# A chain of 1/sqrt moved from GpSimd to VectorE, with GpSimd's row scatters issued in one run

## Chip, cores and metric

One core of a Trainium2 chip. The metric is the device time of one execution in microseconds; the number shown for a kernel is the median of its runs.

## What is computed

The input x is 8 sequences of 512 tokens of 256 values. All of the work starts from xn, the layer norm of x (no gain or bias).

- Recurrence branch: q = xn Wq, v = xn Wv; a state per channel, state[t] = lam * state[t-1] + v[t] with lam = sigmoid(beta) per head; y = q * state; **layer norm of y over its 256 channels, (y - mean) / sqrt(var + 1e-5)**, then gain ln_g and bias ln_b; times silu(xn Wg); times Wo. Its result is s.
- Expert branch: a router picks 2 of 8 experts for each of the 4096 tokens, with softmax weights; each expert is silu(a) * b of a 256 to 1024 projection, then 512 to 256. The sum and a bias go through silu. Its result is g.
- Output: x + s * g.

The change is about the 1/sqrt of the norm in bold.

## The kernel before

One program drives five engines by hand: each engine has its own list of instructions (a queue in program order) and waits on semaphores of the others. Products are split in f16 high and low parts, three matmuls each (L944). A chunk is one sequence: 4 tiles of 128 tokens; CH = 8 chunks. The work has three stages.

**First**, x is loaded and normed in eight groups (the inverse roots of these norms come from GpSimd's `rstd`, L367 to L374, and stay there in both kernels), the router chooses experts, and VectorE works out for each token and each of its two experts a row of a buffer in memory, `slots_dram`. GpSimd then writes the normed rows there: 64 indirect DMAs of 128 rows (`scatter`, L398 to L406; the DMA is L403). The second half of them waits for `routed` to reach 2.

**The early recurrence** runs chunks 0 to 5 (EARLY = 6). Each engine has a function `recur(c)`, chunks 0 and 1 written out and 2 to 5 in a loop:

- VectorE (L791): the scan over 512 steps from PSUM (L798, two instructions), y = q * state (L806), the product with the gate of the chunk before and its low part (`times_gate`, L841 and L844, two instructions each), the statistics of y (`bn_stats` L818, `bn_aggr` L825, which raises `y_var`), in chunk 1 the list of expert blocks (`list_blocks`, L769 to L785), and the low parts of four pieces of expert weights (L832).
- ScalarE (L578): gain and bias of the chunk before (L548), high part of its product (L557), silu of the gate (L586), four weight pieces (L561), then, once `y_rstd` is there, the norm of y from PSUM into z (L597, four instructions), which raises `z_ready`, and the copy of the finished s (L566).
- TensorE: the projections, the transposes of y (L1045) and of z (L1012), the output projection of the chunk before.
- SyncE loads the weight pieces, fills the padding of `slots_dram`, and then waits for `pads_filled` and for all 64 scatters before the first slot load (L309).
- GpSimd works off its scatters and stops for each chunk's root. This order is written out by hand:

```
done = SCATTERS_FIRST
scatter(0, done)
for c in range(EARLY):
    if c >= 1:
        pool.wait_ge(z_ready, c)
    rstd(0, y_var, c + 1, y_rstd)
    end = min(done + SCATTERS_EACH, N_SCATTERS)
    scatter(done, end)
    done = end
```

SCATTERS_FIRST is 14 and SCATTERS_EACH is 11. `rstd` is four small operations on 128x4 elements (L370 to L373; L372 is the power -0.5) and writes the scale and the offset that L597 reads.

**The expert blocks**: 39 blocks of 256 rows, each loaded from `slots_dram` by SyncE, transposed and split (L608 on ScalarE, L854 on VectorE), put through its expert by TensorE, and scattered by GpSimd into `y_dram` (L449). Block 0 needs all 24 weight pieces (L832) and its own L854. VectorE also waits for all 64 row scatters ahead of its first L854.

**The tail** runs chunks 6 and 7 of the recurrence, now without weight pieces, while SyncE loads the experts' results in eight loads of 1 MB (L333). Sums of the two results per token: GpSimd for chunks 1 to 4 (`sum_y`, L477), VectorE for 0, 5, 6 and 7 (L900). ScalarE takes silu (L576), VectorE the product with s (`finish`, L907 and L912), and x is added by GpSimd for chunks 0 to 5 (`add_x`, L473), by VectorE for 6 and 7 (L919). SyncE stores each chunk. On GpSimd the order in the tail is: root of chunk 6, the four sums, root of chunk 7, the six adds. On VectorE: recur(6), L900 and L907 of chunk 0, recur(7), L907 of 1 to 3, L900 of 5 and 6, `times_gate`, the rest.

Lines of the kernel that the change and the prediction touch: L369 to L373, L403, L409 to L417, L477, L480 to L485, L473 on GpSimd; L798, L806, L818, L825, L832, L841, L844, L900, L907 on VectorE; L597 on ScalarE.

Of the kernel before, what the change touches and what calls it, by code (L numbers as in the profile page):

```python
# [33 lines left out]
P = 128  # L34
# [4 lines left out]
TPC = S // P  # L39
CH = B  # L40
# [28 lines left out]
N_SCATTERS = TOPK * NT  # L69
SCATTERS_FIRST = 14  # L70
SCATTERS_EACH = 11

# [9 lines left out]
def build(nc, x, wq, wv, wg, wo, beta, ln_g, ln_b, router, w_exp, bias, out):  # L82
    ctx = ExitStack()
    with ctx:
        def sb(name, shape, dt=F32):
            return ctx.enter_context(nc.sbuf_tensor(name, shape, dt))

        def sem(name):
            return ctx.enter_context(nc.semaphore(name))
# [108 lines left out]
        cols = sb("cols", [P, 4, KD])  # L198
        neg_half = sb("neg_half", [P, TPC])
        spare = sb("spare", [P, 7])  # L200
        bn = [sb(f"bn{i}", [P, TPC, 6]) for i in range(AHEAD)]
# [19 lines left out]
        def slots_ps_of(b, i):  # L221
# [30 lines left out]
            sem, ("sil_ready", "g_ready", "g_hi_ready", "g_split"))  # L252
        meta_ready = sem("meta_ready")
        y_scattered = [sem(f"y_scattered{i}") for i in range(2)]
# [89 lines left out]
        def _(pool):  # L344
# [63 lines left out]

            done = SCATTERS_FIRST  # L409
            scatter(0, done)  # L410
            for c in range(EARLY):
                if c >= 1:
                    pool.wait_ge(z_ready, c)
                rstd(0, y_var, c + 1, y_rstd)
                end = min(done + SCATTERS_EACH, N_SCATTERS)
                scatter(done, end)
                done = end  # L417

# [56 lines left out]
            def sum_y(c):  # L475
                pool.wait_ge(y_loaded[c], 16)
                pool.tensor_tensor(res[c], y_in[c][:, :, 0, :], y_in[c][:, :, 1, :], ALU.add)\  # L477
                    .then_inc(pool_sum, 1)

            for c in range(EARLY, CH):  # L480
                pool.wait_ge(z_ready, c)
                rstd(0, y_var, c + 1, y_rstd)
                if c == EARLY:
                    for early in SUMS_POOL:
                        sum_y(early)  # L485
            for c in range(X_POOL):
# [159 lines left out]
        def _(dve):  # L646
# [142 lines left out]
            dve.wait_ge(lam_ready, 1)  # L789

            def recur(c, convert=True, buffers=early_buffers):  # L791
                states, _, _, _ = buffers
# [31 lines left out]
                for j in range(TPC):  # L824
                    last = dve.bn_aggr(mv[0][:, j, :], bn[0][:, j, :])  # L825
                last.then_inc(y_var, 1)
                if isinstance(c, int) and c == 1:
                    list_blocks()
# [339 lines left out]
```

## Time and profile before

| | |
|---|---|
| median of 3 runs | 570.37 us (569.82 to 572.63) |
| span of the profiled execution | 547.8 us |
| the profiled execution's own time | not given with the profile; the runs are 22.0 to 24.8 us above the span |
| busy share of the span | TensorE 85%, VectorE 60%, GpSimd 50%, ScalarE 41% |
| mean granted TensorE clock | 0.945 |
| row scatters (L403) | 64, 74.0 us busy |
| chain that ended last, by engine | issue 32%, GpSimd 23%, TensorE 17%, DMA 16%, VectorE 7% |

The span is from the first to the last instruction. Busy counts the time in which an engine executes an instruction; waits on semaphores, register work and the issue of DMAs do not count. A length of an instruction in the timeline holds the time that it waits for a port. An engine's idle time before an instruction is put down to what ended it ("[6.53 <-POOL stat L373]"). "issue" is time in which the engine waited for nothing that the profile shows.

### The profile page before, as it was taken

To read this page: it belongs to the slowest core of one execution; us is meant where nothing else is said; L and a number is where in the kernel's file an instruction comes from. 1 tells how busy PE (TensorE), PEld (TensorE's weight loads), DVE (VectorE), ACT (ScalarE), POOL (GpSimd) and SP (SyncE) were. 2 spreads that over 40 slices of the span, in tenths; PEclk is the share of its full clock that TensorE was granted. 3 is DMA by queue.
4 is the path that set the end of the run, shared out by engine and by line. 5 is a ranking of instruction groups with operands and counts; after the bars stand their busy time and mean duration, and the time that the engine had idled before them with its cause. 6 is when DMAs were issued, how large, how long until landed. Compare 5 with 4: busy or idle time off the path is not lost.

```text
span 547.8 us, 13251 instructions
## 1 busy us (share of the span) xinstructions
PE 466.4 (85%) x3896; PEld 377.0 (69%) x3897; DVE 326.6 (60%) x583; ACT 224.5 (41%) x354; POOL 273.9 (50%) x547
## 2 busy tenths in 40 slices
PE   1866668679689899999999999999999999999521
PEld 1753345344468788888888888888888888866321
DVE  4998896578635444554544545545445455448976
ACT  4963337455753333333332433423324333316450
POOL 4617887878722434344343443443444434445784
PEclk9999797799889999999999999999999999999756
DMA  8803659565440324312122121121221211019644
GB/s 261 276 4 108 221 175 313 218 228 176 150 143 20 106 83 153 96 45 68 52 73 58 58 66 58 56 68 48 76 58 56 74 57 39 20 44 370 242 153 153
DMA packets 42051, 64.69 MB, mean 118 GB/s; under 512 B 5037, under 2 KB 30768, under 8 KB 42032
## 3 DMA queue, kind: packets, MB, share of 16 engines
q1 hardware_dynamic: 33408, 46.34, 26.9%
q0 software_dynamic: 6816, 16.92, 8.7%
q10 hardware_dynamic: 1808, 1.19, 0.7%
q8 instruction: 9, 0.15, 0.1%
q14 instruction: 10, 0.08, 0.0%
HBM read 40.93 MB, written 25.33 MB: 121 GB/s over the span
## 4 chain that ended last, share of the span: by engine, by line
issue 32%; POOL 23%; PE 17%; DMA 16%; DVE 7%; POOLq 2%; ACT 2%; DVEq 0%; SPq 0%; ACTq 0%
DMA y_dram<-rows_raw 13%; POOL slots_dram L403 9%; PE bankC L944 5%; PE bankB L944 5%; PE bankA L944 4%; POOL stat L372 2%; POOL y_dram L449 2%; DMA w_raw<-x_in 2%; DVE w_raw L841 1%; POOL rows_raw L436 1%; POOL rows_raw L440 1%; POOL spare L432 1%; PE bankD L1012 1%; POOL rows_raw L428 1%; POOL spare L447 1%
## 5 line engine op out<-in xcount | busy, mean ns | idle before, releaser
L944 PE MATMUL bankA<-rows_raw,w_raw 128*128 128x256 f16 x936 | 110.2, 275 | 2.0 <-DVE rows_raw L854 2.0
L944 PE MATMUL bankC<-w_raw,rows_raw 128*128 x936 | 109.2, 273 | 0.4 <-DVE rows_raw L862 0.3
L944 PE MATMUL bankB<-rows_raw,w_raw 128*128 128x256 f16 x936 | 108.6, 273 | 0.0
L944 PEld LDWEIGHTS bankA<-rows_raw,w_raw 128*128 x936 | 92.0, 99 | 14.1 <-issue 2.7
L944 PEld LDWEIGHTS bankC<-w_raw,rows_raw 128*128 128x128 f16 x936 | 90.0, 98 | 14.3 <-issue 2.6
L944 PEld LDWEIGHTS bankB<-rows_raw,w_raw 128*128 x936 | 91.5, 98 | 10.3
L449 POOL DMA_INDIRECT y_dram<-rows_raw x78 | 79.2, 1015 | 32.8 <-issue 32.8
L403 POOL DMA_INDIRECT slots_dram<-rows_raw,pos_i x64 | 74.0, 1156 | 30.9 <-issue 20.1
L862 DVE TENSOR_TENSOR rows_raw<-rows_raw 128x512 f16<-128x512 f32 x78 | 54.0, 693 | 55.7 <-ACT rows_raw L622 55.7
L859 DVE SCALAR_TENSOR_TENSOR rows_raw<-rows_raw,bankA 128x512 f32<-128x512 f32 x39 | 26.8, 687 | 92.9 <-ACT rows_raw L617 92.9
L617 ACT ACTIVATE rows_raw<-bankA 128x512 f32<-128x512 f32 x39 | 23.3, 597 | 128.5 <-PE bankA L944 128.5
L622 ACT ACTIVATE rows_raw<-rows_raw 128x512 f16<-128x512 f32 x78 | 49.1, 630 | 60.2 <-DVE rows_raw L859 60.2
L447 POOL TENSOR_TENSOR spare<-spare 128x1 f32<-128x1 f32 x39 | 7.5, 192 | 100.1 <-DVE rows_raw L872 100.1
L428 POOL TENSOR_TENSOR rows_raw<-rows_raw,blk_e 128x2 f32<-128x2 f32 x39 | 7.2, 186 | 62.1 <-DMA y_dram<-rows_raw 62.1
L872 DVE SCALAR_TENSOR_TENSOR rows_raw<-bankC,rows_raw 128x256 f32<-128x256 f32 x78 | 34.2, 479 | 4.9 <-PE bankC L944 3.8
L1012 PE MATMUL bankD<-ident,work 128*128 128x128 f32 x64 | 13.5, 381 | 27.2 <-ACT work L597 27.2
L859 DVE SCALAR_TENSOR_TENSOR rows_raw<-rows_raw,bankB 128x512 f32<-128x512 f32 x39 | 26.8, 687 | 16.0 <-ACT rows_raw L617 16.0
L617 ACT ACTIVATE rows_raw<-bankB 128x512 f32<-128x512 f32 x39 | 23.3, 597 | 24.0 <-PE bankB L944 24.0
L597 ACT ACTIVATE work<-bankD,stat 128x256 f32<-128x256 f32 x32 | 15.4, 563 | 41.2 <-POOL stat L373 41.2
L1012 PEld LDWEIGHTS bankD<-ident,work 128*128 128x128 f32 x64 | 10.9, 197 | 30.3 <-ACT work L597 29.9
L832 DVE SCALAR_TENSOR_TENSOR w_raw<-work,w_raw 128x1024 f32 (+1 forms) x24 | 27.6, 1212 | 0.0
L854 DVE TENSOR_TENSOR rows_raw<-bankD,rows_raw 128x512 f16<-128x512 f32 x38 | 26.0, 683 | 0.2 <-ACT rows_raw L608 0.2
(151 smaller groups left out, 670.4 us busy)
## 6 DMA issues: line engine op xcount, KB each, us to landing
work<-w_exp_in SPq DMA_DIRECT2D x24, 512.0 KB, 5.2
rows_raw<-slots_dram SPq DMA_DIRECT2D x39, 260.0 KB
w_raw<-y_dram SPq DMA_DIRECT2D x8, 1024.0 KB, 14.1
w_raw<-x_in SPq DMA_DIRECT2D x9, 512.0 KB, 4.2
out<-w_raw SPq DMA_DIRECT2D x8, 512.0 KB, 2.9
work<-x_in SPq DMA_DIRECT2D x7, 512.0 KB, 4.6
slots_dram<-fill SPq DMA_DIRECT2D x9, 260.0 KB, 4.9
y_dram<-rows_raw POOLq DMA_INDIRECT x78, 2.4
```

The costliest lines, as they stand in the source:

```text
L403: pool.indirect_dma_start(out=slots_dram, out_offset=bass.IndirectOffsetOnAxis(slot, 0), in_=row, in_offset=None, bounds_check=SLOTS - 1, ...
L449: pool.indirect_dma_start(out=y_dram, out_offset=bass.IndirectOffsetOnAxis(dest[i][:, s:s + 1], 0), in_=ys[i][:, s, :], in_offset=None, bo ...
L597: last = act.activation(z[:, j, :], bankD[:, j // 2, j % 2 * D:j % 2 * D + D], ACT.Identity, bias=stat[0][:, 2, j:j + 1], scale=stat[0][:, ...
L617: act.activation(sil[j], AB[j][:, :, 0:BLOCK], ACT.Silu, scale=1.0 / WSCALE).then_inc(sil_ready, 1)
L622: act.activation(g_hi[i][:, 2 * j:2 * j + 2, :], g32[j], ACT.Copy)\
L832: dve.scalar_tensor_tensor(w_lo[:, piece], wst[:, i % STAGES, :], WSCALE, w_hi[:, piece], ALU.mult, ALU.subtract).then_inc(w_lo_ready, 1)
L854: dve.tensor_tensor(xT[i][:, KD:2 * KD, :], slots_ps_of(b, i), xT[i][:, 0:KD, :], ALU.subtract).then_inc(slot_lo_ready, 1)
L859: dve.scalar_tensor_tensor(g32[j], sil[j], 1.0 / WSCALE, AB[j][:, :, BLOCK:2 * BLOCK], ALU.mult, ALU.mult).then_inc(g_ready, 1)
L862: dve.tensor_tensor(g_lo[i][:, 2 * j:2 * j + 2, :], g32[j], g_hi[i][:, 2 * j:2 * j + 2, :], ALU.subtract).then_inc(g_split, 1)
L872: last = dve.scalar_tensor_tensor(ys[i][:, s, :], bankC[:, i, s * D:s * D + D], gate_c[i][:, s:s + 1], half_bias, ALU.mult, ALU.add)
L944: last = pe.matmul(out_ap, lhsT, rhs, start=(n == 0), stop=(n == len(todo) - 1))
L1012: last = pe.transpose(bankD[:, m, j * P:j * P + P], z[:, j, m * P:m * P + P], ident32[:, :])
```

## The change

GpSimd no longer computes the 1/sqrt of the recurrence, neither in the early stage nor in the tail. It issues all 64 scatters in one run. VectorE computes the root in a new function `inverse_root(c)`, called in `recur` right behind `bn_aggr`, ahead of the block list and of the weight pieces. It is a guess from the bits of the number (0x5F3759DF minus half of the bits, as integers) and three Newton steps of three operations each: 12 operations, each followed by a wait on the semaphore `root_step`, and a thirteenth for the offset, which raises `y_rstd`. Ahead of them VectorE waits for `y_var` (raised by itself) and for `z_ready` of the chunk before, for chunk 0 for the last `x_norm`. On GpSimd the four sums of the tail follow the last expert scatter, and the adds follow the sums.

```diff
--- before.py
+++ after.py
@@ -67,8 +67,9 @@
 ROWS_OUT = TOPK * T
 NO_ROW = float(ROWS_OUT + 1)
 N_SCATTERS = TOPK * NT
-SCATTERS_FIRST = 14
-SCATTERS_EACH = 11
+NEWTON = 3
+ROOT_STEPS = 3 + 3 * NEWTON
+SEED = float(0x5F3759DF)
 
 
 def repeat(eng, peeled, end, stride, body):
@@ -197,6 +198,7 @@
         fill32 = sb("fill32", [P, ROW])
         cols = sb("cols", [P, 4, KD])
         neg_half = sb("neg_half", [P, TPC])
+        root = sb("root", [P, 2, TPC])
         spare = sb("spare", [P, 7])
         bn = [sb(f"bn{i}", [P, TPC, 6]) for i in range(AHEAD)]
         mv = [sb(f"mv{i}", [P, TPC, 2]) for i in range(AHEAD)]
@@ -250,7 +252,7 @@
             sem, ("slot_t_ps", "slot_hi_ready", "slot_lo_ready", "h_ps", "y_ps", "y_sb"))
         sil_ready, g_ready, g_hi_ready, g_split = map(
             sem, ("sil_ready", "g_ready", "g_hi_ready", "g_split"))
-        meta_ready = sem("meta_ready")
+        meta_ready, root_step = sem("meta_ready"), sem("root_step")
         y_scattered = [sem(f"y_scattered{i}") for i in range(2)]
         y_loaded = [sem(f"y_loaded{c}") for c in range(CH)]
         pool_sum, moe_sum, moe_silu, gated, pool_added, dve_added = map(
@@ -406,15 +408,7 @@
                         bounds_check=SLOTS - 1, oob_is_err=False).then_inc(rows_scattered, 16)
 
 
-            done = SCATTERS_FIRST
-            scatter(0, done)
-            for c in range(EARLY):
-                if c >= 1:
-                    pool.wait_ge(z_ready, c)
-                rstd(0, y_var, c + 1, y_rstd)
-                end = min(done + SCATTERS_EACH, N_SCATTERS)
-                scatter(done, end)
-                done = end
+            scatter(0, N_SCATTERS)
 
             n_meta = n[0]
 
@@ -477,12 +471,8 @@
                 pool.tensor_tensor(res[c], y_in[c][:, :, 0, :], y_in[c][:, :, 1, :], ALU.add)\
                     .then_inc(pool_sum, 1)
 
-            for c in range(EARLY, CH):
-                pool.wait_ge(z_ready, c)
-                rstd(0, y_var, c + 1, y_rstd)
-                if c == EARLY:
-                    for early in SUMS_POOL:
-                        sum_y(early)
+            for early in SUMS_POOL:
+                sum_y(early)
             for c in range(X_POOL):
                 add_x(c)
 
@@ -788,6 +778,32 @@
 
             dve.wait_ge(lam_ready, 1)
 
+            def inverse_root(c):
+
+                v, y, bias = stat[0][:, 0, :], stat[0][:, 1, :], stat[0][:, 2, :]
+                half, part_y = root[:, 0, :], root[:, 1, :]
+                done = [0]
+
+                def then(ins):
+                    done[0] += 1
+                    ins.then_inc(root_step, 1)
+                    dve.wait_ge(root_step, c * ROOT_STEPS + done[0])
+
+                dve.wait_ge(y_var, c + 1)
+                if isinstance(c, int) and c == 0:
+                    dve.wait_ge(x_norm, CH)
+                else:
+                    dve.wait_ge(z_ready, c)
+                then(dve.tensor_scalar(v, mv[0][:, :, 1], EPS, None, ALU.add))
+                then(dve.tensor_single_scalar(half.bitcast(I32), v.bitcast(I32), 1, ALU.logical_shift_right))
+                then(dve.tensor_scalar(part_y.bitcast(I32), half.bitcast(I32), -1.0, SEED, ALU.mult, ALU.add))
+                for i in range(NEWTON):
+                    then(dve.scalar_tensor_tensor(half, part_y, -0.5, part_y, ALU.mult, ALU.mult))
+                    then(dve.tensor_tensor(half, half, v, ALU.mult))
+                    then(dve.scalar_tensor_tensor(y if i == NEWTON - 1 else part_y, half, 1.5, part_y,
+                                                  ALU.add, ALU.mult))
+                dve.scalar_tensor_tensor(bias, mv[0][:, :, 0], -1.0, y, ALU.mult, ALU.mult).then_inc(y_rstd, 1)
+
             def recur(c, convert=True, buffers=early_buffers):
                 states, _, _, _ = buffers
                 later = not isinstance(c, int) or c >= 1
@@ -824,6 +840,7 @@
                 for j in range(TPC):
                     last = dve.bn_aggr(mv[0][:, j, :], bn[0][:, j, :])
                 last.then_inc(y_var, 1)
+                inverse_root(c)
                 if isinstance(c, int) and c == 1:
                     list_blocks()
                 for i in range(PIECES if convert else 0):
```

## Rows read from the trace of the kernel before

**Rows 1.** Stage, length, busy us of PE, PEld, DVE, ACT, POOL; clock, DMA, GB/s.

```profile
40.00:153.00 113.00, 80.94 (x496) 48.49 (x493) 84.19 (x160) 57.36 (x79) 88.89 (x94) 0.88 0.58 195
153.00:487.00 334.00, 329.59 (x2960) 289.06 (x2959) 164.51 (x272) 116.24 (x198) 130.87 (x382) 1.00 0.22 66
487.00:548.00 61.00, 32.73 (x184) 20.70 (x184) 46.86 (x51) 23.40 (x32) 37.19 (x21) 0.75 0.62 216
```

**Rows 2.** Timeline, chunks 2 and 3: start, length (us), engine, line, operation, [idle before].

```profile
90.51 1.42 DVE L818 BATCH_NORM_STATS2 bn<-bankD 128x6 f32<-128x256 f32 x4 [0.77 <-PE bankD L1045]
...
92.27 4.62 DVE L832 SCALAR_TENSOR_TENSOR w_raw<-work,w_raw 128x1024 f32 x4
...
96.80 2.32 DVE L798 TENSOR_TENSOR_SCAN work<-cols,bankA 128x512 f32<-128x512 f32 x2
...
99.08 0.24 POOL L370 TENSOR_SCALAR stat<-mv 128x4 f32<-128x4 f32 x1
...
99.23 1.23 DVE L806 SCALAR_TENSOR_TENSOR work<-bankB,work 128x1024 f32<-128x1024 f32 x1
...
101.05 1.93 ACT L597 ACTIVATE work<-bankD,stat 128x256 f32<-128x256 f32 x4 [6.53 <-POOL stat L373]
...
101.56 1.10 POOL L403 DMA_INDIRECT slots_dram<-rows_raw,pos_i  x1 [0.54 <-issue]
...
105.94 1.36 DVE L841 TENSOR_TENSOR work<-work 128x512 f32<-128x512 f32 x2 [5.48 <-ACT work L548]
...
107.33 1.36 DVE L844 TENSOR_TENSOR work<-work 128x512 f16<-128x512 f32 x2
```

**Rows 3.** Timeline of VectorE, small chained operations of the routing.

```profile
49.09 0.17 DVE L758 TENSOR_TENSOR w_raw<-w_raw 128x8 f32<-128x8 f32 x1
49.29 0.43 DVE L759 TENSOR_SCALAR w_raw<-w_raw 128x8 int32<-128x8 f32 x1
49.76 0.17 DVE L760 TENSOR_SCALAR w_raw<-w_raw 128x8 int32<-128x8 int32 x1
```

**Rows 4.** Lines L832 and L403: min/median/max ns, first and last start (us).

```profile
L832 DVE SCALAR_TENSOR_TENSOR w_raw<-work,w_raw x24: 1191/1217/1222, 55.6 to 150.5; 128x1024 f32 x16, 128x1024 f16<-128x1024 f32 x8
...
L403 POOL DMA_INDIRECT slots_dram<-rows_raw,pos_i x64: 967/974/4780, 39.5 to 144.5; - x64
```

**Rows 5.** Timeline of VectorE, chunk 1: first row of the block list, and what follows.

```profile
71.67 0.45 DVE L769 TENSOR_TENSOR w_raw<-w_raw 128x312 f32<-128x312 f32 x1
...
74.60 4.61 DVE L832 SCALAR_TENSOR_TENSOR w_raw<-work,w_raw 128x1024 f16<-128x1024 f32 x4
```

**Rows 6.** Timeline, hand-over to the blocks: first slot load, first L854.

```profile
147.94 0.39 SPq L309 DMA_DIRECT2D rows_raw<-slots_dram  x1
...
152.07 0.69 DVE L854 TENSOR_TENSOR rows_raw<-bankB,rows_raw 128x512 f16<-128x512 f32 x1 [0.33 <-ACT rows_raw L608]
```

**Rows 7.** Timeline of GpSimd, chunk 1: the longest scatter.

```profile
75.29 4.78 POOL L403 DMA_INDIRECT slots_dram<-rows_raw,pos_i  x1 [0.30 <-issue]
```

**Rows 8.** Timeline of the tail, VectorE and ScalarE.

```profile
498.71 1.19 DVE L900 TENSOR_TENSOR w_raw<-w_raw 128x1024 f32<-128x1024 f32 x1
...
506.43 3.81 DVE L841 TENSOR_TENSOR w_raw<-w_raw,work 128x512 f32<-128x512 f32 x2 [0.46 <-ACT w_raw L548]
...
510.17 3.43 DVE L844 TENSOR_TENSOR w_raw<-w_raw 128x512 f16<-128x512 f32 x2
...
519.96 1.93 ACT L597 ACTIVATE work<-bankD,stat 128x256 f32<-128x256 f32 x4 [4.36 <-POOL stat L373]
...
528.73 3.44 DVE L844 TENSOR_TENSOR w_raw<-w_raw 128x512 f16<-128x512 f32 x2
```

**Rows 9.** Line L477, as rows 4.

```profile
L477 POOL TENSOR_TENSOR w_raw<-w_raw x4: 2349/2571/2796, 502.3 to 509.7; 128x1024 f32<-128x1024 f32 x4
```

**Rows 10.** DMA issues of 491.9 to 492.3, then 492.3 to 492.9 us; last: landing.

```profile
w_raw<-y_dram SPq DMA_DIRECT2D x1, 1024.0 KB, 8.1
...
w_raw<-y_dram SPq DMA_DIRECT2D x2, 1024.0 KB, 9.8
```

## The prediction, made before the changed kernel was run

> **What bounds the kernel now.** I read first how the time splits by stage [rows 1]. From 153 to 487 us the expert blocks keep TensorE busy 329.6 of 334 us at full clock; the change touches nothing there, so that stage only moves as a whole. The two other stages are the early recurrence (to 153 us, six chunks) and the tail (from 487 us, two chunks). There no engine is full: in the early stage GpSimd is busy 88.9 of 113 us, VectorE 84.2, TensorE 80.9. So the question is who waits for whom within one chunk, and the timeline of chunk 2 answers it [rows 2]. VectorE has the variance at about 92.3 us, when L832 starts behind it. GpSimd looks at it at 99.08 (L370), when its 11 scatters are through, and ScalarE's normalisation L597 starts at 101.05 after 6.53 us of waiting for GpSimd. VectorE pays one step later: L841 of chunk 3 stands still 5.48 us before it starts at 105.94. The period of a chunk is GpSimd's queue: 11 scatters of 1.28 us, a stop of 2.5 us for the root (99.08 to the next L403 at 101.56) and some 2 us of waits in the scatters, 18.6 us together.
>
> **The root on VectorE.** Each chunk gets 13 operations on 128x4 elements, 12 of them followed by a wait on their own semaphore. Small chained operations of this kind stand in the routing [rows 3]: L758 and L759 start at 49.09 and 49.29, so 0.20 us a step, and L758 and L760 are 0.17 us long. 12 x 0.205 + 0.17 + 0.07 for the first wait = 2.7 us, which I take as R. Lower end 2.3 (nothing but the 0.17 us themselves); upper end 3.5, if each of the three one-input steps takes L759's 0.43 instead of 0.17 us. The waits of chunks 2 to 5 hold a loop register, which no row prices by itself; I cost it at nothing, since the register work can run while the step before is executing, and its upper end lies inside that 3.5.
>
> **The early stage.** Without GpSimd a chunk is VectorE's own queue. Start to start in rows 2: L841 to L844 1.39, L844 1.36, L818 to L832 1.76, R, L832 to L798 4.53, L798 to L806 2.43, L806 1.23: 12.7 + R = 15.4 us. What has to stay under that: ScalarE, with 57.4 us for five and a half chunks [rows 1], 10.4 each, and TensorE, whose 80.9 us must fit into some 103. The first L832 group begins at 55.6 [rows 4] and moves to 55.6 + R. Five chunks follow, chunk 1 with the block list, 74.60 - 71.67 = 2.93 us more [rows 5], then the last group of four, 4.6 us: 55.6 + R + 5 x (12.7 + R) + 2.93 + 4.6 = 126.6 + 6R = 142.8 us. Today it ends at 151.7 (last start 150.5 + 1.22), and the first block's L854 starts at 152.07 [rows 6]. New: 142.9, a gain of 9.2 us.
>
> **The scatters** must not be later. L854 waits for them through the slot load that is issued at 147.94 [rows 6]: it starts 7.6 us after the last scatter does (144.5, [rows 4]). Free of all stops they go every 1.28 us (0.97 long in the median [rows 4], 0.30 of issue in front [rows 7]): 39.5 + 63 x 1.28 = 120.1. Of the 24.4 us that the last one is later today, five stops of 2.5 are roots; 12 remain and are for the most part waits for VectorE: beside L832 one scatter took 4.78 us [rows 7]. Those stay, and the root's own steps add little (0.4): 132.5, and L854 could start at 140.1. VectorE is later (142.9), with 2.8 us between them. Lower bound: no waits at all, last start 120.1, which gains nothing, since VectorE then sets L854. Upper bound: GpSimd shut out of each of five L832 groups for 3.8 us, as that once today: 120.1 + 19 + 3 = 142.1, L854 at 149.7.
>
> On that the Trainium skill (SBUF — State Buffer, "Who interferes with whom") has the opposite: a VectorE operation with two SBUF inputs would not stop the writing of descriptors, only a two-port mode would. By it the scatters would end at the lower bound and the rival on them would fall. The 4.78 us row beside L832, which has two SBUF inputs, speaks against it.
>
> **The tail** is where it costs. There GpSimd has roots, sums and adds, and its tensor operations hold VectorE's two-input operations off for their whole length: L841 and L844 are 0.69 us each in the early stage [rows 2], but two of each take 3.81 and 3.43 us in the tail [rows 8], while four L477 of 2.35 us ran [rows 9]. Today GpSimd does the root of chunk 6 first and starts those sums at 502.3. Free of it, it starts each when its data land: the second load, issued at 492.0, lands 8.1 us later, at 500.1; the third, issued about 492.45, by the mean of the two (9.8) after 11.5, at 504.0 [rows 10]. The root of chunk 6 starts at 498.8, where L900 starts today, has 7 of 13 steps done by 500.2, waits for one whole L477 to 502.55, and finishes at 503.8, before the next sum. So L900 waits from 498.7 to 503.7. Carried on: ScalarE's silu (about 1.1) and L597 (1.93) to 508.0, L907 to 508.2 behind the second sum, scan and product (2.4 + 1.2) to 511.8, then L841 and L844 alternate with the fourth sum and with the first add of x, which now comes this early: done 517.4, statistics 519.05. The root of chunk 7 meets an idle GpSimd: ready at 521.75, against L597 at 519.96 [rows 8]. After it VectorE has 3 products, 2 sums, 2 L841 and 2 L844 (5 x 1.17 + 4 x 0.69 = 8.6 us), GpSimd three adds of 2.35, one after the other with little overlap: L844 ends near 536.5 against 528.73 + 3.44 = 532.2. The rest follows as today. Cost of the tail: +4.3 us; between +3.6 (no step of the root caught) and +5.1 (L900 caught behind the second sum too).
>
> **Sum.** -9.2 + 4.3 = -4.9 us on a span of 547.8. The page does not give that execution's own time; the median of the runs is 570.37, so 22.6 us lie around the span if it was a median run, and they stay. 570.4 - 4.9 = 565.5.
>
> **Rivals.**
> (a) The root's one-input steps each wait for a scatter in flight. For: L759, with a scatter beside it, took 0.43 [rows 3]. Against: L760 took 0.17, and it is of the same sort. 3 x 0.26 x 6 = 4.7 us: 570.2, no change. 0.15. A sentence of the same page of the skill bears on it: a two-port mode, which one-input operations can enter, holds the port against any GpSimd instruction.
> (b) Slower: the scatters end the stage. The place is L403 behind L832 and the root: if GpSimd gets in neither between the four L832 nor between the steps, each of five chunks costs it 5 us: 120.1 + 25 + 2.3 = 147.4, L854 at 155.0, so +2.9 + 4.3: 577.6. It decides once the last scatter starts after 143.1. For: the 4.78 us row. Against: 12 us of waits over five chunks today are half of that. 0.10.
> (c) TensorE, at 0.88 of its clock here [rows 1], gives a period of 16.0 instead of 15.4: 3.0 us, 568.5. Against: 81 us of work in 103. 0.10.
> (d) The tail costs nothing, because small steps and L900 slip in and the sums that start 2 us earlier pay back: 561.2. The alternation in rows 8 speaks against it. 0.07.
> The forecast keeps 0.58.
>
> **Numbers.** A measurement tells about 0.5% from no change: 567.5 to 573.2. Faster: the forecast, (d) and a little of (c), 0.65; same: (a), most of (c) and the edge of the forecast, 0.24; slower: (b) and a bad end of (a), 0.11. The range runs from 562.0 (R at 2.3, L854 at 140.1, tail at 3.6: 570.4 - 12.0 + 3.6) to 572.5, which holds (a), (c) and a scatter end at 149.7 with the tail's 4.3; it leaves out (b) and most of (d).
>
> **What would show it.** Right: L597 of chunks 2 to 5 starts 2.7 us behind the variance and 15.4 us after the one before, L841 there no longer waits for ScalarE, all L403 stand in one run whose last starts near 132.5, L854 near 143, the block stage 334 us as before, and in the tail the root of chunk 6 is 5 rather than 2.7 us long with an L477 beside it. Wrong: a step pitch above 0.25 us, a last scatter after 135.3 (then it and not VectorE sets L854), or a tail as long as today's.

## The result, and the profile after

The changed kernel takes 594.15 us in the median of four runs (587.83 to 599.38), the kernel before 570.5 in the runs beside it: a ratio of 1.038, 95% interval 1.033 to 1.043. It is slower; 565.5 was forecast, 562.0 to 572.5 the range. Ratios, here and below, leave out executions in a slower state that any kernel shows now and then (here the one of 599.38 us), so they need not equal the quotient of the medians. The profiled execution of after is the shortest of the four: 587.83 us, with a span of 586.1 against 547.8.

First the stages, with the columns of [rows 1] (VectorE's last group of weights ends, and the blocks begin, at 183 us here and at 153 before):

```profile
40.00:153.00 113.00, 64.99 (x364) 34.87 (x365) 66.92 (x172) 38.97 (x54) 71.89 (x64) 0.76 0.48 158
...
183.00:520.00 337.00, 330.86 (x2960) 289.71 (x2960) 165.05 (x273) 115.38 (x196) 129.70 (x373) 0.99 0.22 65
520.00:586.00 66.00, 33.44 (x184) 20.51 (x184) 54.82 (x78) 23.14 (x32) 32.09 (x14) 0.76 0.57 199
```

In the first 113 us after the same start every engine is busier before than after. Nobody is the bound: something stands still. VectorE's timeline shows where (start, length, engine, line, operation, [idle before <- who ended it]; "remote": the view can name no instruction as the releaser):

```profile
39.85 1.22 DVE L662 TENSOR_TENSOR xs_raw<-bankB,xs_raw 128x1024 f16<-128x1024 f32 x1
72.42 0.29 DVE L687 TENSOR_REDUCE w_raw<-bankD 128x16 f32<-128x128 f32 x1 [31.35 <-remote]
...
76.39 0.37 DVE L698 TENSOR_TENSOR w_raw<-w_raw 128x16 f32<-128x16 f32 x1
85.16 2.33 DVE L814 TENSOR_TENSOR_SCAN work<-cols,bankA 128x512 f32<-128x512 f32 x2 [8.40 <-remote]
...
96.94 4.62 DVE L849 SCALAR_TENSOR_TENSOR w_raw<-work,w_raw 128x1024 f16<-128x1024 f32 x4
...
160.93 0.17 DVE L797 TENSOR_SCALAR stat<-mv 128x4 f32<-128x4 f32 x1
163.31 0.16 DVE L805 SCALAR_TENSOR_TENSOR stat<-mv,stat 128x4 f32<-128x4 f32 x1
163.57 4.63 DVE L849 SCALAR_TENSOR_TENSOR w_raw<-work,w_raw 128x1024 f32 x4
168.12 2.33 DVE L814 TENSOR_TENSOR_SCAN work<-cols,bankA 128x512 f32<-128x512 f32 x2
...
183.42 0.69 DVE L871 TENSOR_TENSOR rows_raw<-bankB,rows_raw 128x512 f16<-128x512 f32 x1
```

L687 begins the second top-2 choice and waits for TensorE's last logits; L814 is the scan of chunk 0 (L798 before) and waits for TensorE's v projection; L849 is the first group of expert weights (L832 before). Two pauses, 31.35 and 8.40 us, stand in code that the diff doesn't touch. The rest is as the change meant it: the root takes 160.93 to 163.57, 2.64 us, with ScalarE and GpSimd no longer in the chain. TensorE's timeline in the same stretch:

```profile
38.95 2.51 PE L981 MATMUL bankD<-rt,xs_raw 128*128 128x8 f16 x71
41.66 0.29 PE L981 MATMUL bankD<-rt,xs_raw 128*128 128x8 f16 x6 [0.20 <-issue]
42.43 0.27 PE L981 MATMUL bankD<-rt,xs_raw 128*128 128x8 f16 x5 [0.48 <-issue]
...
45.43 0.23 PE L981 MATMUL bankD<-rt,xs_raw 128*128 128x8 f16 x3 [0.55 <-issue]
...
50.21 0.38 PE L961 MATMUL bankA<-xs_raw,wat_lo 128*128 128x512 f16 x1
76.80 0.29 PE L990 MATMUL bankD<-w_raw 128*128 128x128 f16 x1 [26.21 <-issue]
```

L981 are the 96 small matmuls that make logits. The first 71 run without a gap, then they drip, some five every 0.75 us. The last stands at 45.43, yet VectorE, which waits for its signal, goes on at 72.42, and the v projection is done at 50.59, yet its reader, free from 76.76 on, starts at 85.16. So by their rows both pieces of work are done, and their signals come 27 and up to 35 us late. The trace's own records of the semaphores say the same: of the logits' signals the seventh stands at 45.44 and the eighth at 72.40, 0.02 us ahead of L687, and that of the v projection at 85.07. No recorded signal of ScalarE comes more than 0.01 us behind the end of its instruction. In the profile of before, none of TensorE's does either. The Trainium skill (Perfetto Trace Analysis, "Summary: the profiler window per engine type") lists the propagation of a semaphore among what the reported windows of VectorE, ScalarE and TensorE hide, and TensorE's end as an estimate; the rows agree, a matmul row says nothing of when its reader hears of it.

GpSimd in that time:

```profile
39.56 1.24 POOL L405 DMA_INDIRECT slots_dram<-rows_raw,pos_i  x1 [10.50 <-DVE rows_raw L727]
...
79.51 0.97 POOL L405 DMA_INDIRECT slots_dram<-rows_raw,pos_i  x1 [0.30 <-issue]
93.49 0.97 POOL L405 DMA_INDIRECT slots_dram<-rows_raw,pos_i  x1 [13.01 <-DVE rows_raw L727]
...
116.17 5.52 POOL L405 DMA_INDIRECT slots_dram<-rows_raw,pos_i  x1 [0.30 <-issue]
...
142.81 0.98 POOL L405 DMA_INDIRECT slots_dram<-rows_raw,pos_i  x1 [0.30 <-issue]
```

The 32 scatters of the first half go out every 1.28 us from 39.56 to 80.5, and the drip begins 2 us after the first. Then GpSimd itself waits 13 us for the second half of the routing. The other 32 are one run too, from 93.49 to 142.81, but on average 1.59 us apart (beside VectorE's work one of them took 5.52 us), and though TensorE's signals are up to 6.7 us late there, VectorE has one pause of over 1 us for them, of 1.49 us. So a long run need not hold VectorE up; the first one did.

**Where the time went, trace against trace.** The rows of before for the same places (VectorE: the choice, the scan of chunk 0, the last gate of the blocks), none of them with a pause ahead:

```profile
42.06 0.29 DVE L697 TENSOR_REDUCE w_raw<-bankD 128x16 f32<-128x128 f32 x1 [1.05 <-PE bankD L964]
...
46.03 2.39 DVE L798 TENSOR_TENSOR_SCAN work<-cols,bankA 128x512 f32<-128x512 f32 x2
...
486.21 0.88 DVE L872 SCALAR_TENSOR_TENSOR rows_raw<-bankC,rows_raw 128x256 f32<-128x256 f32 x2 [2.36 <-PE bankC L944]
```

The first L854/L871 stands at 183.42 for 152.07, +31.35; from it to the last gate of the blocks (L889 at 519.90, before 486.21) 336.48 for 334.14, +2.34; from there to the end 66.20 for 61.59, +4.61. Together 38.3. Inside the first: the scan of chunk 0 starts 39.1 later (85.16 for 46.03), and from it to the blocks it is 7.8 us shorter (98.26 for 106.04).

But 38.3 us of span don't fit 23.7 us of time. That is the first question of the experiments.

### The profile page after: what moved, and what is told of

The parts are those of the page before. It is cut to its first block, busy times and chain, and to the rows that moved or that the text cites. A ratio compares the mean times of both kernels' runs of the same rounds, so it can differ in the third digit from the quotient of the medians.

```text
span 586.1 us, 13373 instructions
## 1 busy us (share of the span) xinstructions
PE 473.3 (81%) x3896; PEld 376.9 (64%) x3897; DVE 346.2 (59%) x687; ACT 224.4 (38%) x354; POOL 253.0 (43%) x515
## 4 chain that ended last, share of the span: by engine, by line
issue 30%; DVE 18%; DMA 18%; POOL 11%; PE 9%; another core or an unknown queue 7%; SPq 2%; POOLq 2%; ACT 2%; DVEq 0%; ACTq 0%
DMA y_dram<-rows_raw 13%; PE bankB L961 3%; PE bankC L961 3%; PE bankA L961 3%; DVE w_raw L849 2%; POOL y_dram L443 2%; DMA w_raw<-x_in 2%; DVE w_raw L924 2%; DVE w_raw L917 2%; DMA work<-w_exp_in 1%; DMA rows_raw<-slots_dram 1%; DVE bn L834 1%; DVE work L814 1%; DVE root L801 1%
## 5 line engine op out<-in xcount | busy, mean ns | idle before, releaser
L961 PEld LDWEIGHTS bankB<-rows_raw,w_raw 128*128 x936 | 91.5, 98 | 10.2
L405 POOL DMA_INDIRECT slots_dram<-rows_raw,pos_i x64 | 72.3, 1130 | 42.4 <-DVE rows_raw L727 23.5
L889 DVE SCALAR_TENSOR_TENSOR rows_raw<-bankC,rows_raw 128x256 f32<-128x256 f32 x78 | 34.2, 480 | 5.1 <-PE bankC L961 4.0
L849 DVE SCALAR_TENSOR_TENSOR w_raw<-work,w_raw 128x1024 f32 (+1 forms) x24 | 27.8, 1217 | 0.4
L1087 PE MATMUL bankD<-ident,rows_raw 128*128 128x128 f32 x152 | 23.8, 279 | 3.7 <-DMA rows_raw<-slots_dram 3.5
L871 DVE TENSOR_TENSOR rows_raw<-bankD,rows_raw 128x512 f16<-128x512 f32 x38 | 26.0, 684 | 0.2 <-ACT rows_raw L598 0.2
L467 POOL TENSOR_TENSOR w_raw<-w_raw,work 128x1024 f32<-128x1024 f32 x6 | 18.7, 3126 | 14.3 <-DVE w_raw L924 14.3
```

The lines of the kernel that those rows point to most:

```text
L405: pool.indirect_dma_start(out=slots_dram, out_offset=bass.IndirectOffsetOnAxis(slot, 0), in_=row, in_offset=None, bounds_check=SLOTS - 1, ...
L467: pool.tensor_tensor(res[c], res[c], x_of(c), ALU.add).then_inc(pool_added, 1)
L849: dve.scalar_tensor_tensor(w_lo[:, piece], wst[:, i % STAGES, :], WSCALE, w_hi[:, piece], ALU.mult, ALU.subtract).then_inc(w_lo_ready, 1)
L871: dve.tensor_tensor(xT[i][:, KD:2 * KD, :], slots_ps_of(b, i), xT[i][:, 0:KD, :], ALU.subtract).then_inc(slot_lo_ready, 1)
L889: last = dve.scalar_tensor_tensor(ys[i][:, s, :], bankC[:, i, s * D:s * D + D], gate_c[i][:, s:s + 1], half_bias, ALU.mult, ALU.add)
L961: last = pe.matmul(out_ap, lhsT, rhs, start=(n == 0), stop=(n == len(todo) - 1))
```

## The experiments

Ratios are to the kernel before on the same chip, with their 95% intervals. The spans are those of the profiled execution.

**The kernel before by itself.** No edit.

> The kernel before, unchanged, to see what its executions look like one by one. The profiled execution of before has a span of 547.8 us, while its runs take 569.8 to 572.6; the changed kernel's executions are only 1.7 us longer than their spans (587.83 against 586.1). Theory A: a part of the executions of before stands still for some 20 us as the changed kernel does, and the profiled one is without it; then spans of about 568 to 571 appear, and with a profile of one of them a pause of some 20 us. Theory B: the 22.6 us lie around the span; then the spans stay at 547 to 549.

570.9 us, 1.001 (0.998 to 1.004), span 568.5, 1.7 us less than that execution's time. Theory A holds: the profile that stood ahead of the prediction is of an execution some 20 us shorter than usual. In all the comparisons that follow, repeats of before took 563 to 575 us (but for two of 1661.8 and 1661.9, whose cause is not known), none near the 549.5 that its span would give. VectorE's timeline of an ordinary one, then TensorE's:

```profile
60.08 0.29 DVE L697 TENSOR_REDUCE w_raw<-bankD 128x16 f32<-128x128 f32 x1 [18.73 <-remote]
```

```profile
39.47 1.44 PE L964 MATMUL bankD<-rt,xs_raw 128*128 128x8 f16 x51
41.18 0.42 PE L964 MATMUL bankD<-rt,xs_raw 128*128 128x8 f16 x11 [0.27 <-issue]
...
48.60 0.29 PE L964 MATMUL bankD<-rt,xs_raw 128*128 128x8 f16 x5 [1.20 <-issue]
50.04 1.02 PE L944 MATMUL bankA<-xs_raw,wat_hi 128*128 128x512 f16 x2 [1.14 <-issue]
```

The same drip, the same late signal, only shorter. L697 goes on at 60.08; the last of the 14 scatters starts at 56.75. Against this execution the changed kernel's 17.6 us of span (586.1 for 568.5) add up: the scan of chunk 0 starts 21.1 later (85.16 for 64.04), from it to the blocks it takes 10.2 less (98.26 for 108.43), the blocks take 2.1 and the tail 4.6 more. The changed kernel's other three executions, 4 to 12 us longer, have no profile.

**Scatters paced as before, roots on VectorE.**

```diff
-            scatter(0, N_SCATTERS)
+            scatter(0, 14)
+            for c in range(EARLY):
+                pool.wait_ge(y_rstd, c + 1)
+                scatter(14 + 11 * c, min(25 + 11 * c, N_SCATTERS))
```

> The changed kernel, its roots on VectorE as they are, but GpSimd's scatters stop where they stopped before: 14, then 11 after each root. Theory 1 (the uninterrupted run of scatters holds back the signals from TensorE to VectorE, the pauses of 31.4 and 8.4 us): both pauses go, the early stage has the pitch of 15.2 us per chunk, the span falls by 35 to 42 us to 544 to 551. Rival 2 (VectorE's longer program is the cause, 389 instructions in place of 312): the pause of 31 us stays, the span stays at 580 or more.

583.9 us (573.67 to 587.99), 1.024 (1.017 to 1.031). VectorE's timeline:

```profile
59.95 0.29 DVE L690 TENSOR_REDUCE w_raw<-bankD 128x16 f32<-128x128 f32 x1 [18.76 <-remote]
```

In the profiled execution, the shortest (span 571.9), the first pause is 18.8 us, to 59.95: that of the kernel before, with VectorE's longer program. Rival 2 falls. My number, a span of 544 to 551, fell too, since the kernel before has that pause itself. The three other repeats took 580.9 to 588.0 us; they have no profile, so what held them is not known.

**First run of 32 scatters, GpSimd's own roots** (`SCATTERS_FIRST = 32` in the kernel before).

> The kernel before, its roots on GpSimd as they were, but the first run of scatters is 32 long in place of 14 (all that the first half of the routing gives). The first root then waits until 80 us by the issue pitch of 1.28 us, about 20 us later than now. Theory 1 (the run of scatters holds back signals to other engines): VectorE also stands still from 41 us until past 60 us ahead of the second top-2 choice. Rival 2 (VectorE's program): VectorE goes on at 42 us and at 46 us as before, and waits only for the root of chunk 0.

585.1 us, 1.027 (1.019 to 1.035). VectorE's timeline:

```profile
80.78 0.29 DVE L697 TENSOR_REDUCE w_raw<-bankD 128x16 f32<-128x128 f32 x1 [39.79 <-remote]
```

VectorE's pause is 39.79 us, to 80.78, and the 32nd scatter starts at 79.40. No root has moved here: the longer run alone makes the longer pause.

**At most four scatters in flight** (four semaphores in turn, each scatter waits for the one four before it).

> The changed kernel with a wait ahead of each scatter, until the one four before it has landed (four semaphores in place of one). GpSimd has no other stop. Theory 1a (what holds the signals back is that GpSimd's queue runs far ahead, 14 scatters and more): the pauses of 31.4 and 8.4 us go, the span is 544 to 552. Theory 1b (it is the back-to-back scatters themselves, not how many are queued): the pauses stay, the span stays above 580.

588.9 us, 1.031 (1.027 to 1.035), pause 43.8 us, to 84.99, with the 32nd scatter at 79.48. The first 32 scatters still come every 1.28 us, so the wait never bound: each had landed before the fourth behind it came up. There was no queue running far ahead to cut back, and Theory 1a falls with that.

**First runs of 7 and of 2** (`SCATTERS_FIRST` 7 and 2, `SCATTERS_EACH` 12 and 13, in the kernel before).

> The kernel before, its first run of scatters 7 long in place of 14 (and 12 in place of 11 behind each root), no other wait. If the pause ahead of the second top-2 choice ends with the first run of scatters (60.1 us with 14, 80.8 with 32), VectorE goes on at about 51 us here (39.9 + 7 x 1.28 + 2.3), the pause is 10 us in place of 18.7, the span 560. Rival 2 (the pause has nothing to do with the length of the run): it stays at 18.7 us.

> The same with a first run of 2 scatters (and 13 behind each root). By the same rule VectorE goes on at 44 to 45 us (39.9 + 2 x 1.28 + 2.3) and chunk 0 can then have its root at once; the span would fall to 549 to 553, if the 62 other scatters, 13 behind a root at 16.6 us with the root's own 3 to 4 us, don't become what chunks wait for (19.7 x 5 from about 59 us puts the last at 155, and the span at about 552 to 556).

VectorE's timeline with a first run of 7, then of 2:

```profile
49.67 0.29 DVE L697 TENSOR_REDUCE w_raw<-bankD 128x16 f32<-128x128 f32 x1 [8.69 <-remote]
```

```profile
43.18 0.29 DVE L697 TENSOR_REDUCE w_raw<-bankD 128x16 f32<-128x128 f32 x1 [2.15 <-PE bankD L964]
```

The four lengths of the first run side by side, from VectorE's and GpSimd's timelines:

| first run | last scatter of it starts | VectorE goes on | its pause |
|---|---|---|---|
| 2 | 41.08 | 43.18 | 2.15 |
| 7 | 47.45 | 49.67 | 8.69 |
| 14 | 56.75 | 60.08 | 18.73 |
| 32 | 79.40 | 80.78 | 39.79 |

(The changed kernel's 32: 79.51 and 72.42, let through before the end, then held again.) Yet neither kernel is faster than the one before: 570.1 us with 7, 1.003 (1.000 to 1.005), and 568.5 us with 2, 1.003 (0.999 to 1.007). What the pause gives back, GpSimd's queue takes: with two scatters ahead, its 62 others and the roots give a period of about 20.8 us (L370's stops stand before the scatters at 84.95, 106.11, 126.86), and the last scatter starts at 159.68. In the kernel before, the pause was partly free: GpSimd used it for 14 scatters.

**First scatter only after the route matmuls**, in the changed kernel, in the kernel before, in the changed kernel with its last two roots on GpSimd, and in the changed kernel with stops:

```diff
+            pool.wait_ge(logits_done, CH)
             scatter(0, N_SCATTERS)
```

> The changed kernel, with one wait more: GpSimd starts its first scatter only when TensorE has finished all the route matmuls (the eighth signal), about 42 us instead of 39.6. Theory 3: what goes wrong is that the scatters start in the middle of the dense run of 96 route matmuls (27 ns each); TensorE then drips, and its signal to VectorE comes only with the end of the run of scatters or late in it (60.1 with 14 scatters, 80.8 with 32, 72.4 in the changed kernel). Then both pauses go (31.4 and 8.4 us), the second top-2 choice starts at 42 us, and the prediction's own sums hold from there: the low half of block 0's rows is made at 143 to 146 us, the tail has its extra 4 to 5 us, span 543 to 547, time 545 to 549. Rival 4: signals from TensorE are held whenever scatters run back to back, whatever TensorE does; then the signal of the v projection is held until the first 32 scatters are out at about 83 us, and the span stays above 575.

> The kernel before, with the same one wait ahead of its first scatter. Theory 3: its usual pause of 18.7 us goes, the span falls from 568.5 to 548 to 551, the time from 570.9 to 550 to 553. Rival 4 (held whenever scatters run): the pause moves to the v projection, the span stays at 566 to 571.

> As e4_after_route_first, but the roots of the last two chunks (6 and 7, behind the blocks) are GpSimd's power again, with its sums and additions of the tail behind them as before. By the tail's term of the prediction (4.3 us; the traces show 66.2 us from the last gate of the blocks to the end, against 61.6) it is 4 to 5 us shorter than e4_after_route_first. Rival (the tail's loss comes from elsewhere, as from DMA landings): within 1 us of e4_after_route_first.

> The changed kernel with the wait of e4_after_route_first and the stops of e1_paced_scatters: 14 scatters, then 11 after each root. It tells what the uninterrupted issue is worth once the pause is gone. If the scatters are never last (the prediction: last start at 132.5, and it decides only above 135.3), it is within 1 us of e4_after_route_first, or slower by up to 3 us, since the last group of scatters can start only after the root of chunk 4 at about 128 us and its 6 scatters end near 136. Rival: back-to-back scatters still cost signals in the chunks, then it is faster than e4_after_route_first by 2 us or more.

In all four the choice starts at 42.7 to 43.2 us after a wait of 1.4 or less: the first pause is gone. What follows differs. The kernel before gains: 557.2 us, 0.980 (0.977 to 0.983). The changed kernel's four repeats took 552.82, 570.57, 600.27 and 610.85 us, so no ratio is given; with GpSimd's late roots too they spread, from 566.87 to 606.59. With stops it is 571.4 us, 1.006 (1.002 to 1.010). Lines of VectorE and of TensorE in the 610.85 us execution:

```profile
133.21 1.43 DVE L835 BATCH_NORM_STATS2 bn<-bankD 128x6 f32<-128x256 f32 x4 [48.15 <-remote]
```

```profile
83.00 1.97 PE L1063 MATMUL bankD<-ident,work 128*128 128x128 f32 x8 [17.23 <-issue]
...
136.70 0.60 PE L962 MATMUL bankC<-wat_hi,work 128*128 128x256 f16 x2 [1.04 <-issue]
```

L835 waits for the transposes L1063, done at 85.0. The semaphore's record has their signal at 133.19; the last of the 64 scatters started at 129.02. In the same stretch a signal of ScalarE is on time: L577 ends at 113.32, and TensorE, which waits for it, goes on at 113.37. TensorE drips again from 113 to 137 and then runs freely. So Theory 3 was half right: with the first scatters behind the route matmuls the first pause goes, but TensorE's later signals can be caught if the run goes on. In this kernel and in the one with stops the run began at 46 us and the first late signals follow L1030/L1033 at 62. In the latter only two stops made gaps, from 78.8 to 88.72 and from 138.3 to 153.17: the others wait for a root that is long there when 11 scatters are through, and GpSimd issued from 88.72 to 138.3 without a break. The kernel before, so treated, has 2.5 to 4.3 us without a scatter at each root, and VectorE's longest pause for a late signal is 3.7 us.

**Rests that are gaps.** Roots 0 to 5 on VectorE, 6 and 7 on GpSimd, first scatter after the route matmuls, and:

```diff
+                    if a % 8 == 0 and a:
+                        pool.wait_ge(rows_scattered, 16 * a)
```

> e6_route_first_pool_tail (early roots on VectorE, late ones on GpSimd, first scatter after the route matmuls) with a rest in GpSimd's issue: ahead of every eighth scatter it waits until all before it have landed. Theory 5 (TensorE's signals are held up only by a run of scatters that goes on for some 15 us or more without a gap, and each gap lets them through): no pause of more than 5 us is left, the repeats lie within 5 us of one another in place of 40, the first low half at 146 to 152 us, span 542 to 550. Rival 4 (back-to-back scatters hold signals at any length): pauses of 5 to 20 us remain, span 560 or more.

564.8 us, 0.994 (0.990 to 0.998), ten repeats within 6.7 us. From 43 to 142.8 us VectorE waits only 1.6 us in all, and no recorded signal of TensorE is more than 0.24 us late:

```profile
112.10 2.32 DVE L821 TENSOR_TENSOR_SCAN work<-cols,bankA 128x512 f32<-128x512 f32 x2
...
127.36 2.32 DVE L821 TENSOR_TENSOR_SCAN work<-cols,bankA 128x512 f32<-128x512 f32 x2
...
166.80 0.69 DVE L879 TENSOR_TENSOR rows_raw<-bankB,rows_raw 128x512 f16<-128x512 f32 x1 [24.01 <-ACT rows_raw L605]
```

The period of a chunk is 15.3 us and VectorE is through with the early stage at 142.8 (166.80 - 24.01). Then it waits 24 us, because the rests put the last scatter at 158.82. The signals are mended, but my span of 542 to 550 is not reached (563.9): I had left out that seven rests cost their landings on GpSimd's queue.

**Rests every 12 and every 16, two scatters ahead of the route matmuls**, and the same two-then-wait in the kernel before.

> e8_rest_every_eight with two scatters ahead of the route matmuls (a first run of two holds nothing up: the choice started at 43.2 us) and a rest after every twelve instead of eight (4 rests more than the first, each 2 to 3 us). In e8_rest_every_eight the recurrence was done at 137 us and the scatters ended last, at 160 us, with the first low half at 166.8. Here the scatters take 45.5 + 62 x 1.28 + 10 to 12 us beside VectorE + 4 x 2.5 = 145 to 148 us, the first low half comes at 152 to 155, span 549 to 552, time 551 to 554. If a run of twelve (16 us) is already long enough to hold signals up, pauses of 5 us or more come back and the repeats spread by more than 10 us.

> The same with a rest after every sixteen scatters (20 us of issue): 2.5 us earlier by the issue alone, span 546 to 549. Theory 5 puts the onset of the held signals at 15 to 17 us of uninterrupted issue (62 us after a start at 46 in e4_after_route_first and in e7_route_first_paced): then pauses show here and not in e11_rest_every_twelve, and the time is 560 or more.

> The kernel before with two scatters, then the wait for the route matmuls, then its order as it was (12 more, then 11 behind each root). e5_before_route_first took 557.2, with GpSimd's queue 6 us later than in the profile of before; two scatters done ahead give 2.6 us back: span 550 to 553, time 552 to 556. If its issue is not what the chunks wait for, it is the same as e5_before_route_first, 557.

554.0 us, 0.978 (0.969 to 0.986); 552.0 us, 0.973 (0.966 to 0.980); and 554.2 us, 0.978 (0.971 to 0.985). All three beat the kernel before by 2 to 3%. With a rest every 16 VectorE has one long pause for a late signal, ahead of the product of chunk 4:

```profile
123.45 1.22 DVE L830 SCALAR_TENSOR_TENSOR work<-bankB,work 128x1024 f32<-128x1024 f32 x1 [5.34 <-remote]
```

VectorE's wait begins at 118.1, 18 us into the run of scatters from 100.39 to 122.0, and ends 1.5 us behind it. The onset is near what Theory 5 had (15 to 17 us), the price of 560 us or more was too high: it came once in this execution, and the four repeats lie within 3.1 us. The first low half stands at 154.88 (VectorE last; its last scatter started at 143.53), against 155.68 with a rest every 12 (scatters last, 146.85) and 152.63 in the kernel before so treated. So with both treated, moving the early roots to VectorE is worth little here: 552.0 and 554.2 us, intervals that overlap. VectorE's own signals can be late as well. Its root of chunk 0 in the version with a rest every 16:

```profile
57.04 0.17 DVE L805 TENSOR_SCALAR stat<-mv 128x4 f32<-128x4 f32 x1
...
58.41 0.16 DVE L811 SCALAR_TENSOR_TENSOR root<-root 128x4 f32<-128x4 f32 x1
59.44 0.17 DVE L809 SCALAR_TENSOR_TENSOR root<-root 128x4 f32<-128x4 f32 x1 [0.87 <-DVE root L811]
...
62.45 0.16 DVE L813 SCALAR_TENSOR_TENSOR stat<-mv,stat 128x4 f32<-128x4 f32 x1
```

It takes 5.57 us in place of 2.55, and 4.40 with a rest every 12, in steps that wait for nothing but VectorE's own step before.

**Gaps and rate, in the run of 32** (GpSimd's roots; a rest before every fourth scatter; six small memsets, each waited for, behind every scatter).

> e2_burst_pool_root (GpSimd's roots as before, first run of 32 scatters), with a rest ahead of every fourth scatter of the first 32, in which all issued ones land. Without rests VectorE stood still until 80.8 us. Theory 5 (a gap in the issue lets TensorE's signals through): VectorE goes on at the first gap, 39.9 + 4 x 1.28 + 2.3 = 47 us, or at the second, 55 us, though the run of scatters, 8 x (5.1 + 2.5), lasts until 100 us. Rival (the signals wait until a count of scatters is through): it stands still until 90 us or later.

> e2_burst_pool_root with six small memsets of GpSimd behind each of the first 31 scatters, each waited for, some 1.2 us together: GpSimd is as busy as before, the scatters come every 2.5 us instead of every 1.28. Theory 6 (it is the rate of scatters): VectorE goes on at 42 to 50 us. Rival (it is GpSimd's uninterrupted queue, whatever is in it): VectorE stands still until the 32 are through, 120 us.

582.5 us, 1.020 (1.006 to 1.033), and 611.3 us, 1.07 (1.05 to 1.09), both long because chunk 0's root waits behind 32 slow scatters. VectorE's choice in each, and TensorE's logits in the second:

```profile
45.83 0.29 DVE L699 TENSOR_REDUCE w_raw<-bankD 128x16 f32<-128x128 f32 x1 [4.63 <-PE bankD L966]
```

```profile
43.96 0.29 DVE L700 TENSOR_REDUCE w_raw<-bankD 128x16 f32<-128x128 f32 x1 [2.37 <-PE bankD L967]
```

```profile
40.40 2.55 PE L967 MATMUL bankD<-rt,xs_raw 128*128 128x8 f16 x96
```

With rests it starts at 45.83, inside the first gap (scatters at 43.82 and 47.09), with 28 still to come. At half rate (scatters every 2.7 us, GpSimd never idle) it starts at 43.96, and TensorE's 96 route matmuls are one run of 2.55 us without a drip. The few signals of TensorE on record in the rest of the slowed stretch (six in each) are on time within 0.01 us. So it is neither a count of scatters nor a GpSimd without idle time, but scatters one behind the other every 1.28 us.

## Why the prediction was wrong

- **The step that failed is the start of the early stage: "The first L832 group begins at 55.6 ... and moves to 55.6 + R".** That is 58.3; it started at 96.94 (L849). Behind it stands "Free of all stops they go every 1.28 us": the sum prices the stops that were taken out as GpSimd's own time, and puts at nothing what an unbroken run does to the other engines. In the runs the stop behind the 14th scatter is what lets TensorE's signal through. Taking it out makes a first run of 32, and the pause ahead of chunk 0 grows from 18.7 us to 31.35 + 8.40; the run of 32 with GpSimd's own roots does the same without the rest of the change. None of my rivals had it; (b) named the scatters as the place, but by their end, not by what they hold up.
- **"22.6 us lie around the span if it was a median run, and they stay"**: it was no such run, and 1.7 lie around it. The profiled execution of before had no pause, while the ordinary one has 18.7 us of it, and all timed ones are about as long as that one. The gap between span and median was there to be asked about: I took it as a constant, and it was the very effect that decides. It didn't change the sum, since I made only a difference, but it hid the mechanism.
- **The root, R = 2.7 us**: 2.64 in chunk 4 to the next instruction, 2.55 in chunk 7, steps of 0.20. Right. Chunks 0, 1 and 2, each with two scatters beside the root, took 2.56, 2.55 and 2.55, so rival (a) falls (the 0.17 us of L760 that I set against it had no scatter beside it: they ran to 49.73 and from 50.03), and the loop register of chunks 2 to 5 cost nothing seen. That a step's own signal can be late, as in the 5.57 us above, was not in the sum; in the changed kernel it shows in the block list, 4.24 us (111.98 to 116.22) for 2.93.
- **The early stage, gain 9.2**: in the changed kernel's own trace 7.8 from the scan of chunk 0 on, with 1.49 us of a late signal in it; the period was to be 15.4 and is 15.23 (152.89 to 168.12). In the version with a rest every eight VectorE ends at 142.8 with 142.8 forecast. Rival (c) falls. Against ordinary executions of before the term is 10.2 us (108.43 to 98.26).
- **Scatters, last start 132.5**: 142.81, and the 13 us for which GpSimd waited at 93.49 explain it: without them it is 129.8, so "12 remain ... Those stay" was about right. Beside L849 one scatter took 5.52 us, as [rows 7] had 4.78; the Trainium skill (SBUF — State Buffer, "Who interferes with whom"), by which two SBUF inputs of VectorE stop only a GpSimd operation that reads SBUF, and the writing of descriptors is inferred to go on, again doesn't agree with the row, unless a scatter counts as such a read because its row numbers lie in SBUF (pos_i); no run here tells. Rival (b)'s mechanism is real once rests are put in: it sets the block stage's start in the versions with rests every 8 and 12.
- **The tail, +4.3**: measured +4.6. By the last gate to the end it is 66.20, 66.08, 65.84, 66.03 and 66.13 us in five kernels with VectorE's late roots, 61.59, 61.63, 61.57 and 61.52 in four with GpSimd's, and 61.60 where the changed kernel got only these two roots back. VectorE's timeline there:

```profile
532.53 0.17 DVE L797 TENSOR_SCALAR stat<-mv 128x4 f32<-128x4 f32 x1
...
533.73 2.34 DVE L801 SCALAR_TENSOR_TENSOR root<-root 128x4 f32<-128x4 f32 x1
...
536.50 2.22 DVE L801 SCALAR_TENSOR_TENSOR root<-root 128x4 f32<-128x4 f32 x1
...
539.23 1.22 DVE L917 TENSOR_TENSOR w_raw<-w_raw 128x1024 f32<-128x1024 f32 x1
...
568.67 1.29 DVE L861 TENSOR_TENSOR w_raw<-w_raw 128x512 f16<-128x512 f32 x2 [0.15 <-ACT w_raw L547]
```

  The mechanism is as written, a small step caught for a whole GpSimd sum (they start at 533.71 and 536.36, 2.35 and 2.34 us), but twice: the root of chunk 6 takes 6.7 us, not 5.0. In the paced kernel, in the one with four in flight and in the paced one with the route matmuls first it was caught once (4.6, 4.6 and 4.7 us), and their tails are as long: 66.08, 65.84 and 66.13 us. So the second catch is not what the tail costs. The last L861 ends 50.1 us after the last gate, for 50.3 forecast. Rival (d) falls.
- **The block stage unchanged**: +2.34. TensorE's granted clock is 0.73 in its first 12 us for 0.86 in the 12 us from 152 before, and its first pass takes 5.15 for 4.35 us. That is 0.8 us of it. The rest is open, but small: over all kernels here, whose block stages are the same, this stretch takes 332.8 to 338.8 us.

## What to carry to other kernels

When the median of the runs and the span of the profile differ by more than the few microseconds of the others, the profile is of another execution than the timed ones: look for what the timed ones do before arguing from it. A stop in a queue of scatters that looks like lost time may be what lets other engines' signals pass; before taking it out, put a run of the new length into the old kernel alone. A short run, a gap of some 2 us in which all has landed after every eighth scatter, or half the rate were enough here; with a gap after every sixteenth one pause came back, and yet that version has the lowest median, 552.0 us: every gap also costs GpSimd time.

## What was not expected of the hardware

- GpSimd's scatters (128 rows of 1040 bytes, 0.97 us long, every 1.28 us) hold up what TensorE signals: by up to 1.2 us with a first run of 2, and so that VectorE stands still for 39.8 us with one of 32 and for 48.2 in a later chunk, until a gap in the run or up to 4.6 us behind its end. TensorE itself issues in small groups meanwhile (some five matmuls per 0.75 us); with scatters at half the rate it issues 96 in 2.55 us, 27 ns each.
- It is TensorE above all. VectorE's own signals come up to 1.8 us late in the changed kernel and up to 3.7 in the version with the route matmuls first and GpSimd's late roots; none of ScalarE's on record is over 0.01 us late in any trace.
- It is not certain in each execution: the profile of before shows a run of 14 with no hold at all, and the changed kernel with the route matmuls first took 552.8 and 610.9 us in two repeats. Nor is it in each run: the changed kernel's second 32 scatters cost VectorE 1.49 us.
- Whether the recording takes part in the hold is open, and it is the rival that is left. The profile of before has 5540 records of signals, and is the only one where no signal of TensorE is over 0.01 us late. Every other trace has far fewer, those with hardly a late signal too: 3946 in the changed kernel, 3910 in the ordinary execution of before, 4363 with a rest every eight. Every execution that has a span beside its time here was recorded, so none shows what happens without. Which part of a scatter does it, its descriptors, its writes or its 16 landing signals, was not tried. A shortage of instructions at TensorE was not tested either; from 36 to 90 us the changed kernel's trace has 3 packets of instruction loads and the profile of before 4, which does not point to it.
